# A decoder layer on one Trainium2 core: all transposing DMAs issued by ScalarE instead of SyncE

## The chip, the core and the metric

The kernel runs on one core of one Trainium2 chip. The metric is the device time of one execution, in microseconds (us); lower is better. Engines are named as the profile names them: PE (TensorE, with its weight loads as PEld), DVE (VectorE), ACT (ScalarE), POOL (GpSimd) and SP (SyncE, which here does nothing but issue DMAs and wait). "SPq" and "ACTq" mark DMA issues.

## What is computed

A pre-norm decoder layer on x of shape (16, 256, 256): 16 blocks (index b) of 256 rows, model width 256. Cut to what matters:

```python
x = x + attn(layernorm(x))            # one head, width 256, causal, linear position bias
x = x + xattn(layernorm(x), ctx)      # 16 heads of 16, keys and values from ctx (16, 256, 256)
x = x + moe(layernorm(x))             # 8 experts, top 2, F = 1024

def moe(x):                           # x: 4096 rows
    p = softmax(x @ w_gate)           # (.., 8); the best two are kept and scaled to sum 1
    g, u = split(x @ w_gate_up[e])    # per expert, 256 -> 2 * 1024
    y = (silu(g) * u) @ w_down[e]     # 1024 -> 256
    return sum of p[e] * y[e] over the two chosen experts
```

All is float32 in and out. Inside, most products are made of float16 halves: a value is split in a high half and the rest, and three products are added.

## The kernel before

It is written directly per engine: five instruction streams, with semaphores between them, and the order in each stream is written out by hand.

**Attention part** (0 to about 490 us). A software pipeline over the 16 blocks: `iteration(b, ...)` on every engine handles the front of block b+2 (norms, self-attention, projections: functions `f_...`), the head work of blocks b and b+1 (`h_...`) and the tail of block b-1 (`t_...`: output projection, third norm, gate logits, top two, and ranks). In the same iterations the expert weights are split into halves (`split_hi` on ACT, `split_lo` on POOL) and stored to memory, three pieces an iteration. The iterations in the loop take 28.2 us each.

The gate of a block needs its normed rows transposed. The path is: variance (DVE) -> `rsqrt_tail` (POOL L767) -> `t_norm3` (DVE L1344) -> `t_xn3`, the high half (ACT L1101, helper L1000) -> `xn3_rest`, the low half (POOL L807, semaphore xn3_lo) -> `transpose_normed` (SP L427 to 434, a transposing DMA of 256 KB from xn3_h to xn3_t) -> `t_gate` (PE L2241, matmul line L2246), which sits at a fixed place between the head matmuls in PE's order. SP also issues all loads and stores in a fixed order around it: `load_pieces`, `store_stream`, `transpose_normed`, `load_next`, `store_pieces`, `stack_rows`, `stack_k_hi` and so on, `store_normed` last.

**Expert part** (about 490 us to the end). The 8192 (row, expert) pairs are sorted into 68 slots of 128 rows; four streams j = 0..3 take slots in turn, so slot s belongs to stream s % 4. For slot s:
- SP loads the slot's entries (L579), DVE makes row numbers (`slot_rows`, L1929), POOL gathers the 128 rows with an indirect DMA (`gather`, L893, semaphore rows_in), SP transposes them with a DMA (`transpose_rows`, L615, semaphore rows_t_in), PE multiplies.
- In SP's `slot(s)` (L656): once PE has finished the gate and up products of slot s (gu_ps), it waits for the gathered rows of slot s+4, issues their transposition, and then loads the weights of slot s+4 (2 MB `load_gate_up` L527, 1 MB `load_down` L531; only where the expert changes), and after that entries for slot s+8. At three points in the loop and once at its end `load_second` loads another 3 MB, for the last four slots.
- PE's `slot` runs four steps f = 0..3; a step is `gate_up(s, f)` (24 matmuls, L2477) and a `down` of two steps earlier (6 matmuls, L2507): after `gate_up(s, 2)` comes `down(s, 0)`, after `gate_up(s, 3)` comes `down(s, 1)`.
- ACT's `slot` (L1276) per step: `silu` of step f (L1282), then `act_round` of step f-1 (L1000, act_hi), and in odd streams a `result` at f = 2 (L1264). DVE makes act_t (L1976) and act_lo (L1923). `down(s, f)` waits for act_lo of step f.
- POOL alternates `gather(s+4)` and `scatter_results(s)` (L913, adds a slot's results to `out` in memory; each waits for the one before to have landed).

Between the two parts stand `before_last` (block 14's heads) and `last_attention` (block 15's), whose tails run in part beside the first slots (`last_tail`).

## Time and profile before

| | us |
|---|---|
| three timed runs | 1106.5, 1101.28, 1106.62 (median 1106.5) |
| the profiled execution | 1098.74, span 1097.0 |
| PE busy | 1003.0 (91%) |
| DVE, ACT, POOL busy | 643.0 (59%), 627.1 (57%), 536.1 (49%) |
| mean granted PE clock | 0.975 of full |

The profile comes from one execution, which is a little faster than the three timed ones. The busy shares are means over two parts that differ: in the attention iterations ACT is busy for nine tenths of the time, in the expert part for under four tenths. Such shares say little of a change in one place; the stretches and the waits in the section on rows are what to read. In a timeline a line is: start, duration, engine, source line, operation, output <- input, count, and in brackets the engine's idle time before it with what ended it. DMA issues show the time in which the issuing engine writes them out, not the transfer.

### The profile page before, as it was taken

What the parts mean: (1) busy time and instruction counts of PE and PEld (TensorE: products, weight loads), DVE (VectorE), ACT (ScalarE), POOL (GpSimd) and SP (SyncE); (2) the same over time, 40 slices, a digit from 0 to 9 for tenths busy, and PEclk for the clock granted to TensorE, in tenths of its full rate; (3) what the DMA queues carried; (4) which work ended last, traced back from release to release, by engine and by line L of the source; (5) the groups of instructions that cost most, each with busy time, mean ns of one, the idle gap of its engine ahead of it and who ended that gap; (6) DMA issues with size and microseconds to landing.
All of it is one profiled execution on the core that took longest, in us unless ns stands there. A gap on an engine that the chain in (4) does not pass through costs nothing.

```text
span 1097.0 us, 36445 instructions
## 1 busy us (share of the span) xinstructions
PE 1003.0 (91%) x12720; PEld 834.7 (76%) x12720; DVE 643.0 (59%) x2077; ACT 627.1 (57%) x1343; POOL 536.1 (49%) x580
## 2 busy tenths in 40 slices
PE   5689899999999999765999999999999999999984
PEld 4356666666666666423988999999999999999974
DVE  6667788888888887752456444444444444444422
ACT  6589898988888888644343333333333333334321
POOL 6756777777777777413244232233323232333313
PEclk9799999999999999987999999999999999999998
DMA  5855656656666663359543455854664752235791
GB/s 191 269 179 177 161 173 183 184 188 186 192 192 192 193 194 118 108 138 285 165 70 49 62 157 166 265 132 93 170 160 98 231 161 52 48 52 158 231 301 18
DMA packets 146817, 173.95 MB, mean 159 GB/s; under 512 B 75072, under 2 KB 123264, under 8 KB 141888
## 3 DMA queue, kind: packets, MB, share of 16 engines
q1 hardware_dynamic: 131486, 154.95, 45.9%
q0 software_dynamic: 15248, 18.18, 9.9%
q8 instruction: 35, 0.57, 0.3%
q14 instruction: 30, 0.25, 0.1%
q10 hardware_dynamic: 18, 0.01, 0.0%
HBM read 270.75 MB, written 43.07 MB: 286 GB/s over the span
## 4 chain that ended last, share of the span: by engine, by line
PE 61%; DVE 12%; DMA 11%; issue 7%; POOL 4%; ACT 2%; another core or an unknown queue 1%; SPq 1%; DVEq 0%; ACTq 0%; POOLq 0%
PE front L2477 14%; PE t_ring L2477 14%; PE pv L2507 7%; PE s_ring L2507 7%; DMA out<-y_sb,place_i 5%; DMA xn_t<-xn_h 4%; PE pv L2204 3%; PE front L2045 3%; PE s_ring L2171 3%; PE front L2054 2%; PE t_ring L2189 2%; DVE nmax L1417 2%; DVE stats L1326 2%; POOL entries L770 1%; POOL xn_h L807 1%
## 5 line engine op out<-in xcount | busy, mean ns | idle before, releaser
L913 POOL DMA_INDIRECT out<-y_sb,place_i x64 | 100.3, 1568 | 279.4 <-ACT y_sb L1264 81.0
L2477 PE MATMUL t_ring<-rows_t,wgu_sb 128*128 128x128 f16 x3072 | 194.0, 220 | 0.0
L2477 PE MATMUL front<-rows_t,wgu_sb 128*128 128x128 f16 x3072 | 192.5, 219 | 0.0
L2477 PEld LDWEIGHTS t_ring<-rows_t,wgu_sb 128*128 128x128 f16 x3072 | 183.8, 98 | 2.9
L2477 PEld LDWEIGHTS front<-rows_t,wgu_sb 128*128 128x128 f16 x3072 | 182.1, 98 | 3.8 <-issue 0.8
L1083 ACT ACTIVATE probs_t<-t_ring,mask_bias 128x512 f32<-128x512 f32 x256 | 164.7, 699 | 31.9 <-PE t_ring L2189 30.1
L1417 DVE TENSOR_REDUCE nmax<-s_ring 128x2 f32<-128x512 f32 x256 | 166.0, 685 | 14.5 <-PE s_ring L2171 12.3
L1282 ACT ACTIVATE silu_g<-t_ring 128x256 f32<-128x256 f32 x136 | 52.3, 385 | 169.4 <-PE t_ring L2477 152.1
L1282 ACT ACTIVATE silu_g<-front 128x256 f32<-128x256 f32 x136 | 51.9, 383 | 166.1 <-PE front L2477 144.2
L1976 DVE SCALAR_TENSOR_TENSOR act_t<-t_ring,silu_g 128x256 f32<-128x256 f32 x136 | 57.7, 425 | 151.5 <-ACT silu_g L1282 138.0
L1976 DVE SCALAR_TENSOR_TENSOR act_t<-front,silu_g 128x256 f32<-128x256 f32 x136 | 57.6, 424 | 146.4 <-ACT silu_g L1282 142.2
L814 POOL TENSOR_TENSOR w_halves<-w_scaled,w_halves 128x256 f16<-128x256 f32 x192 | 122.3, 670 | 12.1 <-ACT w_scaled L1116 11.8
L1000 ACT ACTIVATE act_hi<-act_t 128x256 f16<-128x256 f32 x272 | 111.5, 410 | 15.6 <-DVE act_t L1976 15.3
L1923 DVE TENSOR_TENSOR act_lo<-act_t,act_hi 128x256 f16<-128x256 f32 x272 | 114.4, 421 | 1.3 <-issue 1.2
L893 POOL DMA_INDIRECT rows<-normed,row_i x68 | 68.3, 1004 | 88.7 <-DVE row_i L1929 59.1
L2507 PE MATMUL pv<-wd_sb,act_hi 128*128 128x256 f16 x512 | 104.8, 273 | 2.3 <-issue 1.1
L2507 PE MATMUL s_ring<-wd_sb,act_hi 128*128 128x256 f16 x512 | 105.5, 274 | 1.6 <-DVE act_lo L1923 1.6
L2171 PE MATMUL s_ring<-k_stack,q_stack 128*128 128x256 f16 x512 | 93.5, 285 | 8.0 <-DVE nmax L1417 4.1
L2189 PE MATMUL t_ring<-q_stack,k_stack 128*128 128x256 f16 x512 | 88.3, 276 | 7.2 <-ACT probs_t L1083 5.8
L2171 PEld LDWEIGHTS s_ring<-k_stack,q_stack 128*128 128x128 f16 x512 | 42.8, 99 | 53.0 <-DVE nmax L1417 27.9
L2204 PE MATMUL pv<-probs_t,v_aug 128*32 128x256 f32 x1024 | 78.3, 398 | 0.0
L791 POOL TENSOR_TENSOR xn_h<-xn_t,xn_h 128x512 f16<-128x512 f32 x32 | 37.4, 1168 | 81.1 <-ACT xn_h L1019 69.0
(307 smaller groups left out, 1855.6 us busy)
## 6 DMA issues: line engine op xcount, KB each, us to landing
wgu_sb<-gu_split SPq DMA_DIRECT2D x68, 2048.0 KB
wd_sb<-down_split SPq DMA_DIRECT2D x68, 1024.0 KB
w_piece<-in_w_gu SPq DMA_DIRECT2D x32, 512.0 KB, 4.6
gu_split<-w_halves SPq DMA_DIRECT2D x32, 512.0 KB, 3.8
w_piece<-in_w_down SPq DMA_DIRECT2D x16, 512.0 KB, 6.3
down_split<-w_halves SPq DMA_DIRECT2D x16, 512.0 KB, 4.4
x_in<-in_x SPq DMA_DIRECT2D x16, 256.0 KB, 2.9
ctx_in<-in_ctx_t_in SPq DMA_DIRECT2D x16, 256.0 KB, 3.0
```

Of the source, the lines that this page charges most:

```text
L814: o = nc.gpsimd.tensor_tensor(w_halves[:, i, 1, c:c + LOCKED], w_scaled[:, i, c:c + LOCKED], w_halves[:, i, 0, c:c + LOCKED], ALU.subtract)
L1000: return nc.scalar.activation(to, frm, ACT.Copy)
L1083: nc.scalar.activation(probs_t[:, g % 2, r], t_ring[r][:].rearrange("p (j q) -> p j q", j=2), ACT.Exp, bias=mask_bias[:, g % 2, bass.ds(b, ...
L1282: nc.scalar.activation(silu_g[:, f % 2], gu_ring[f][:, 0:2 * SLOT], ACT.Silu, scale=1 / (WSCALE * RSCALE)).then_inc(silu_sb, 1)
L1417: nc.vector.tensor_reduce(nmax[:, n // HJ, :, n % HJ], s_ring[n % 2][:].rearrange("p (r k) -> p r k", r=2), AX.X, ALU.max, negate=True).th ...
L1923: nc.vector.tensor_tensor(act_lo[:, f], act_t[:, f % 2], act_hi[:, f], ALU.subtract).then_inc(alo_sb, 1)
L1976: nc.vector.scalar_tensor_tensor(act_t[:, f % 2], gu_ring[f][:, 2 * SLOT:4 * SLOT], ASCALE / (WSCALE * RSCALE), silu_g[:, f % 2], ALU.mult ...
L2171: o = nc.tensor.matmul(s_ring[n % 2][:, r * S:(r + 1) * S], q_stack[:, p, j, qt * P:(qt + 1) * P], k_stack[:, p, r, j], start=True, stop=True)
L2189: o = nc.tensor.matmul(t_ring[r][:, jj * S:(jj + 1) * S], k_stack[:, p, r, 2 * jp + jj, kt * P:(kt + 1) * P], q_stack[:, p, 2 * jp + jj], ...
L2204: o = nc.tensor.matmul(pv[q:q + 32, 0:S], v_aug[:, p, kt, HJ * r + 2 * jp + jj], probs_t[:, g % 2, r, jj], start=(kt == 0), stop=(kt == 1))
L2477: o = nc.tensor.matmul(gu_ring[f][:, part * SLOT:(part + 1) * SLOT], wgu_sb[j][:, w, at:at + P], rows_t[:, j, NC * r + c], start=(i == 0), ...
L2507: o = nc.tensor.matmul(down_banks[j % 2][:, 0:D], a[:, f, k * SLOT:(k + 1) * SLOT], wd_sb[j][:, w, tile_ * D:(tile_ + 1) * D], start=(tile ...
```

## The change

Every transposing DMA leaves SP's stream and goes into ACT's, as `t_turn` (gates) and `turn_rows` (expert rows), with the same waits in front:

```diff
 # ACT
+            def t_turn(c, p):
+                act.wait_ge(xn3_lo, c + 2)
+                act.sem_inc(act_passed, 1)
+                act.wait_ge(gate_ps, c + 1)
+                act.sem_inc(act_passed, 1)
+                nc.scalar.dma_start_transpose(xn3_t[:].rearrange("p t a n -> p (t a) n"),
+                                              xn3_h[:, p].rearrange("p t d -> p (t d)")).then_inc(xn3t_in, 16)
+            def turn_rows(j, g):
+                act.wait_ge(rows_in[j], 16 * g + 16)
+                act.sem_inc(act_passed, 1)
+                nc.scalar.dma_start_transpose(rows_t[:, j], rows[:, j]).then_inc(rows_t_in[j], 16)
 # ACT, iteration
                     h_exp(b, 3, 0)
                     h_exp(b, 3, 1)
+                    h_out(b, p, 0)
                 if c:
                     t_xn3(b - 1, 1 - p, h + p - 1)
-                if t:
-                    h_out(b, p, 0)
                 if f:
                     split_hi(b + 2, 2, p, h + 2)
+                if c:
+                    t_turn(b - 1, 1 - p)
                 if t:
                     h_exp(b, 4, 0)
...
 # ACT, slot: behind silu(s, 1) and act_round(s, 0)
+                    if f == 1 and more:
+                        turn_rows((j - 1) % STREAMS, g + (1 if j else 0))
 # ACT, last_attention and last_tail
+                    if g in (0, 2):
+                        turn_rows(g // 2, 0)
+                    if g == 6:
+                        t_turn(b - 1, 0)
...
+                if s == 0 and f in (2, 3):
+                    turn_rows(f, 0)
+                if s == 3 and f == 2:
+                    t_turn(B - 1, 1)
 # SP, iteration
                     load_pieces(b + 3, h + 1 + p, 1 - p)
-                if c:
-                    store_stream(b - 1)
-                    transpose_normed(b - 1, 1 - p)
                 if f and (not isinstance(b, int) or b + 4 < B):
                     load_next(b + 4, p)
+                if c:
+                    store_normed(b - 1, 1 - p)
+                    store_stream(b - 1)
...
-                if c:
-                    store_normed(b - 1, 1 - p)
 # SP, slot
                     sp.wait_ge(gu_ps, FP * s + FP)
-                    transpose_rows(j, g + 1)
                     load_gate_up(e, j, new)
 # SP, ahead of the slots
             sp.wait_ge(exp_sb, 16 * (B - 1))
-            transpose_rows(0, 0)
-            transpose_rows(1, 0)
...
             load_stream(2)
-            transpose_rows(2, 0)
-            transpose_rows(3, 0)
             load_stream(3)
 # POOL, iteration
+                if parted:
+                    scatter_part(p, 2)
                 if c:
                     rsqrt_tail(b - 1)
-                if parted:
-                    scatter_part(p, 2)
-                    scatter_part(p, 3)
+                if n:
+                    rsqrt_norm1(b + 3)
                 if c:
                     xn3_rest(b - 1, 1 - p)
...
+                if parted:
+                    scatter_part(p, 3)
```

In slot s, ACT thus turns the rows of slot s+3 (stream j-1), at step 1; SP turned those of slot s+4 once slot s had its gate and up products. The order of the iteration is written anew on the other engines too: on PE `h_values`, `h_scores` and `h_scores_t` change places by one or two (the gate product `t_gate` now follows `h_scores_t(5, 1)` and `h_scores(12, 14)`, ahead of `h_values(4)` and `h_scores_t(6, 0)`), on DVE `t_norm3` comes one `h_max` later and the two `t_recip` stand together, on ACT `t_gate` comes ahead of `h_exp(6, ..)`. In the first fronts (the pipeline's filling) weights, copies and loads of blocks 0 and 1 are ordered anew on all engines. No arithmetic is added or removed.

## Rows read from the trace of the kernel before

**Rows 1.** Stretches: length, busy us (and instructions) per engine, PE clock, DMA share, GB/s.
```profile
244.70:272.90 28.20, 27.00 (x257) 18.96 (x255) 23.43 (x76) 25.38 (x48) 21.86 (x27) 1.00 0.65 187
...
481.20:484.00 2.80, 2.76 (x27) 1.29 (x28) 1.53 (x7) 1.48 (x3) 0.77 (x1) 0.50 0.03 11
...
620.00:1020.00 400.00, 400.00 (x6016) 386.35 (x6014) 176.80 (x576) 152.79 (x427) 128.66 (x100) 1.00 0.52 136
```
**Rows 2.** Waits of SP's own queue: us in total, times, longest.
```profile
SPq L614 <- DMA rows<-normed,row_i: 185.9, 49, 10.3
```
**Rows 3.** Single source lines of DMA issues: duration ns min/median/max, first and last start.
```profile
L433 SPq DMA_TRANSPOSE xn_t<-xn_h x16: 1274/1318/3480, 101.0 to 550.5; - x16
...
DMA to landing us min/median/max: 3.1/3.2/10.4
...
L615 SPq DMA_TRANSPOSE rows_t<-rows x68: 1197/1226/3821, 490.7 to 1048.4; - x68
...
L1294 ACTq DMA_DIRECT2D q_stack<-nmax_t x1: 1270/1270/1270, 488.0 to 488.0; - x1
...
L518 SPq DMA_DIRECT2D q_stack<-nmax_t x15: 662/667/727, 57.5 to 453.8; - x15
```
**Rows 4.** Timeline of one attention iteration around the gate's transposition, POOL, ACT, SP.
```profile
243.41 1.18 POOL L807 TENSOR_TENSOR xn_h<-o_n,xn_h 128x512 f16<-128x512 f32 x1
...
244.02 1.06 ACT L1116 ACTIVATE w_scaled<-w_piece 128x1024 f32<-128x1024 f32 x1
...
244.78 1.31 SPq L433 DMA_TRANSPOSE xn_t<-xn_h  x1
```
**Rows 5.** Timeline of PE at three of the 16 gate products.
```profile
248.03 0.46 PE L2246 MATMUL tail<-wg_split,xn_t 128*128 128x8 f16 x12 [0.19 <-DMA xn_t<-xn_h]
...
481.24 0.48 PE L2246 MATMUL tail<-wg_split,xn_t 128*128 128x8 f16 x12 [5.49 <-DMA xn_t<-xn_h]
...
515.14 0.48 PE L2246 MATMUL tail<-wg_split,xn_t 128*128 128x8 f16 x12 [9.05 <-DMA xn_t<-xn_h]
```
**Rows 6.** Timeline of an ordinary slot, steps 1 and 2, all engines.
```profile
840.42 1.00 POOL L893 DMA_INDIRECT rows<-normed,row_i  x1 [0.46 <-issue]
...
842.20 0.41 ACT L1000 ACTIVATE act_hi<-act_t 128x256 f16<-128x256 f32 x1
...
843.25 1.22 SPq L615 DMA_TRANSPOSE rows_t<-rows  x1
...
843.92 0.38 ACT L1282 ACTIVATE silu_g<-t_ring 128x256 f32<-128x256 f32 x1 [1.31 <-PE t_ring L2477]
...
844.67 0.41 DVE L1923 TENSOR_TENSOR act_lo<-act_t,act_hi 128x256 f16<-128x256 f32 x1
...
844.86 0.35 SPq L527 DMA_DIRECT2D wgu_sb<-gu_split  x1
...
845.71 0.27 PE L2507 MATMUL pv<-wd_sb,act_hi 128*128 128x256 f16 x1
```
**Rows 7.** The next slot, whose rows come late: POOL, ACT, SP.
```profile
848.38 1.00 POOL L893 DMA_INDIRECT rows<-normed,row_i  x1 [0.74 <-issue]
...
851.90 0.38 ACT L1282 ACTIVATE silu_g<-t_ring 128x256 f32<-128x256 f32 x1 [1.31 <-PE t_ring L2477]
...
856.56 1.21 SPq L615 DMA_TRANSPOSE rows_t<-rows  x1
```
**Rows 8.** Timeline: an early slot with late rows, SP and ACT.
```profile
577.73 0.38 ACT L1282 ACTIVATE silu_g<-t_ring 128x256 f32<-128x256 f32 x1 [0.98 <-PE t_ring L2477]
...
579.60 1.22 SPq L615 DMA_TRANSPOSE rows_t<-rows  x1
```
**Rows 9.** SP's timeline: first and last transposition with late rows between 620 and 1020.
```profile
641.29 1.24 SPq L615 DMA_TRANSPOSE rows_t<-rows  x1
...
1000.39 1.24 SPq L615 DMA_TRANSPOSE rows_t<-rows  x1
```

160 lines of the change are left out of this document (73 added, 87 removed).

## The prediction

> **What bounds the kernel now.** I read first the stretches, then the waits of SP's queue, then single iterations and slots in the timeline. The stretches [rows 1] show two parts. In an attention iteration of 28.2 us PE is busy for 27.0 and ACT for 25.4: PE sets the pace and ACT stands close behind, with 2.8 us free. From 620 to 1020 PE is busy for all of 400 us, 50 slots of 8.0 us; ACT works 153 us there. So in the expert part nothing but PE matters, as long as nobody keeps PE waiting. SP waited there for gathered rows 49 times, 185.9 us in all and up to 10.3 at once [rows 2], and PE did not notice: SP has nothing behind that wait that is needed within three slots. The change gives this wait to ACT, whose next instruction is the silu that PE needs two microseconds later. That is the centre of the forecast.
>
> **Expert slots, the wait.** In slot s ACT will stand at `turn_rows` after silu of step 1 and act_round of step 0. Take the ordinary slot [rows 6]. ACT is through with that at 842.61 (842.20 + 0.41). The rows were gathered from 840.42 and SP, which waits for nothing else, issued at 843.25; so ACT waits 0.6 us, then issues for 1.22 us, to 844.47. Its silu of step 2 was at 843.92: 0.55 us late. What is late next: act_lo of step 1 ended at 845.08 (844.67 + 0.41) and PE's `down` that needs it began at 845.71, so 0.63 us are free. 0.55 against 0.63: an ordinary slot costs PE nothing, or a tenth or two where act_lo is a little later. For some 35 ordinary slots I enter +2 us.
>
> A late slot is another matter [rows 7]. Its gather was issued at 848.38 and its rows were there only when SP issued at 856.56, 8.2 us later instead of 2.8, beside 3 MB of expert weights issued from 844.86 [rows 6]. ACT would be free of the issue at 857.77, its silu was due at 851.90: 5.87 late, less 0.63 free, 5.2 us of PE standing. PE has only one step of gate and up products to do meanwhile, and that is in the 0.63. The same subtraction over all slots from 620 to 1020 gives nine groups of neighbouring late slots, the first with the issue at 641.29 and the last at 1000.39 [rows 9]; counted by the latest of each group, since once PE has stood the next rows come in time, they are 4.6 to 6.9 us each, **51 us** together. SP will issue a slot's weights some 5 to 7 us earlier, as it no longer waits for the rows. That moves the burst onto the slot's own gather instead of the next one's: a gather begun some 2 us after the weights, as at present one begun 3.5 us after them, is late all the same. I keep nine; between a half (25) and eleven bursts (60).
>
> Before 620 the slots 1 to 9 have late rows for other reasons (POOL has the last tails). At 579.60 SP issued for a slot whose silu of step 2 was at 577.73 [rows 8]: 579.60 + 1.22 - 577.73 - 0.63 = 2.5. Four such slots give 8 to 11; SP itself was late in one, so +6, bounds 0 and 10.
>
> **The clock behind a stop.** After the 5.49 us in which PE waited at 481 [rows 5] the granted clock stood at half in 481.2 to 484.0 [rows 1], so 2.8 us gave 1.4 us of work. Nine stops of like length may each do this. Not all will, as some are shorter: +1 us each, **+9**, bounds 0 and 20.
>
> **Attention iterations.** Removed: SP's wait and issue. Added: the same on ACT. ACT's last activation ahead of it, the third `split_hi`, ends at 245.08; SP issued at 244.78 and needed 1.31 us [rows 4]. On ACT the issue comes right behind, to about 246.3, and the exponentials of group 4 come 1.3 us later. ACT has 2.8 us free an iteration [rows 1], but PE waits for these exponentials, and the new order puts only one or two more score products (0.27 us each) ahead of them. The gate's transposition starts up to 0.5 us later and takes 3.2 us to land [rows 3]; PE's gate product had waited 0.2 us in this iteration [rows 5] and is at about the same place. POOL's single scatter less ahead of `xn3_rest` gains little, because ACT's high half, now behind `h_out`, comes 0.3 us later. Bounds: minus 1.2 (all that PE is idle in an iteration) and plus 1.3 (ACT's issue in full). I take +0.5, nearer to ACT's side, as two engines over 26 of 28.2 us get in each other's way; for 13 iterations **+6.5**, bounds -15 and +17.
>
> The Trainium skill, "Perfetto Trace Analysis", section "Per-engine timelines", says that an engine's sequencer pushes an activation to a queue and goes on to the next instruction, while a DMA is executed by the sequencer. Then the issue would run beside the `split_hi` still at work and the term would be 0 or a gain, the sum 6.5 us lower. No row here shows an ACT issue behind a running activation, so this is not in the sum. In a slot it would change nothing, since ACT is idle there when the rows come.
>
> The other way round: ACT's one DMA issue took 1.27 us, where the same transfer from SP took 0.67 [rows 3]. If transpositions cost ACT 0.6 more than SP's 1.23, every slot goes over its 0.63. That is a rival below.
>
> **Between the parts.** The gate products of blocks 13 and 14 waited 5.49 and 9.05 us [rows 5]. The second wait is for a transposition that stood in SP's queue behind 3 MB of weights, which SP had issued late since it waited for rows first; one such took 10.4 us to land instead of 3.2 [rows 3]. From ACT it doesn't stand behind them, and the weights go 4 to 7 us earlier. Most of the 9.05 should go; late next are ACT's own issues, three of 1.2 us in `last_attention`, and the gathers of rows 2 and 3. Net **-8**, bounds -13 and +3 (the transfer shares the engines with the next weights). At 481 nothing changes. First fronts anew: a different order of the same work, 0, bounds ±3. The end: a chain of result scatters behind the last slots, the same length, 0, bounds ±5.
>
> **Sum.** On the profiled execution's 1098.7: + 6.5 (iterations) - 8 (between) + 6 (early slots) + 2 (ordinary) + 51 (late) + 9 (clock) = 1165.2. The profiled execution lies 2.5 to 8 us under the three timed runs, so I add 3: **1168**.
>
> **Rivals.**
> - *ACT's waits are shorter than SP's were.* Part of the late rows come earlier because results are scattered earlier or the burst misses the gather; half of the late term, no clock loss: 1098.7 + 6.5 - 8 + 6 + 25 + 3 = 1131. For it: the lateness is set by where a burst of 10 us falls against a gather every 8 us. Against: a gather between -1.5 and +5 us of a burst's start was late each time, and the new place is inside.
> - *The rows are in time (the other side).* If the gather lands before ACT is there plus 0.7 us in nearly all slots, the expert part costs nothing; the iterations give back PE's idle 1.2 us each (-15) and the stop between the parts goes (-8): 1098.7 - 23 + 3 = 1079. It decides from there on: late rows under 0.7 us. Against: rows 7 and 9.
> - *ACT issues slowly*, by the 1.27 against 0.67: 0.6 us more in some 58 slots (35) and 13 iterations (8): 1168 + 43 = 1211.
> - *It doesn't tell*: gains between and in the iterations offset a small loss in the slots, 1102 to 1111.
> The Trainium skill, "DMA: Bandwidth & Descriptors", section "Issuing engines are not separate DMA queues", says that starting DMAs on several engines saves only the sequencer's time for it, which is usually small. By it the 186 us of SP's waiting buy nothing; the trace agrees as far as PE was never short of weights from 620 to 1020.
>
> **How the numbers follow.** Forecast 0.58, shorter waits 0.20, slow issue 0.08, the other side 0.09, no difference 0.05. Half a per cent, 5.5 us, is about what a measurement of this kernel can tell from no change. Faster: 0.09. Within 0.5%: 0.05. Slower: 0.86. Range for 8 in 10: from 1115 (shorter waits at their low end) to 1200 (late term 60, clock 20, iterations +12 and ordinary slots +5 over their values).
>
> **What would show it.** Late slots: in the profile after, ACT's silu of step 2 preceded by idle time that a gather's DMA ended, PE idle ahead of `down` behind act_lo for 4 to 7 us some nine times, and PE busy under 0.9 of the expert part. Clock: half level behind these. Iterations: a period of 28.7 us. Between: the gate product of block 14 waiting under 3 us. Wrong would be: PE still busy without a gap from 620 on, or ordinary slots over 8.3 us.

## The result, and the profile after

The changed kernel takes 1276.94 us (median of four runs, 1275.25 to 1283.97) where the kernel before took 1103.89 in the same comparison (1098.99 to 1106.62): a ratio of 1.1585, interval 1.1519 to 1.1652. It was forecast slower, at 1168, with a range to 1200. The direction held; 109 us are missing from the forecast. (One execution of j_gate_first below, 1677.64 us at a granted clock of 0.56, lies apart from its nine others and is in no ratio.) The profiled execution has a span of 1276.3 us, PE is busy for 84% of it and its mean granted clock is 0.917.

The stretches of the profile after, one attention iteration and the expert part that answers to [rows 1]; columns as there:

```profile
301.50:335.60 34.10, 29.76 (x257) 19.99 (x256) 23.84 (x76) 25.66 (x48) 21.85 (x26) 0.90 0.51 155
...
620.00:1020.00 400.00, 351.74 (x4930) 330.04 (x4928) 158.62 (x548) 126.62 (x352) 115.26 (x90) 0.94 0.46 114
```

The same 257 PE instructions that took an iteration of 28.2 us now take 34.1. ACT does hardly more work than before (25.66 against 25.38 us), so it isn't short of time. Of the 5.9 us more, 3.1 are PE idle; 2.8 are PE busy for longer with the same instructions, and its granted clock is 0.90 where it was 1.00. In the expert part PE stands for 48 of 400 us, where it had stood for none.

Three places carry the difference: the iterations, the part between, and the slots. They are measured between the same instructions of both traces: the issues of the gate's transposition of blocks 0 and 13, the first `silu` of slot 0, and the first `silu` of the last slot.

| stretch | before | after | difference | forecast |
|---|---|---|---|---|
| 13 attention iterations | 375.0 | 433.2 | +58 | +6.5 |
| block 13's transposition to slot 0 | 42.3 | 57.2 | +15 | -8 |
| slots 0 to 13 | 114.1 | 133.7 | +20 | +6 |
| slots 13 to 60 | 375.1 | 448.4 | +73 | +62 |
| slots 60 to 67 | 66.5 | 77.1 | +11 | 0 |

(The forecast's 62 are its 51 for late slots, 9 for the clock and 2 for ordinary slots.)

**A late slot.** The timeline after, ACT, POOL, SP and PE of one slot; columns: start, duration, engine, line, what, in brackets the idle time before it and what ended it:

```profile
711.55 0.34 SPq L518 DMA_DIRECT2D wgu_sb<-gu_split  x1
...
714.32 1.01 POOL L871 DMA_INDIRECT rows<-normed,row_i  x1 [0.30 <-issue]
...
716.24 0.41 ACT L978 ACTIVATE act_hi<-act_t 128x256 f16<-128x256 f32 x1
720.56 1.22 ACTq L1260 DMA_TRANSPOSE rows_t<-rows  x1
721.95 0.38 ACT L1281 ACTIVATE silu_g<-t_ring 128x256 f32<-128x256 f32 x1 [5.30 <-issue]
...
723.18 0.39 PE L2510 MATMUL s_ring<-wd_sb,act_hi 128*128 128x256 f16 x1 [3.27 <-DVE act_lo L1923]
```

This is the picture forecast from [rows 7]. (POOL L871 is the gather, L891 the scatter; L1281 is ACT's `silu`, L1260 its `turn_rows`.) The gather was issued 2.8 us behind the weights' issue and came 6.2 us later; ACT was free at 716.65 and issued at 720.56, its `silu` was at 721.95, and PE ran out of work and waited for act_lo. It waited for it 31 times in this part (the waits of PE from 620 to 1180; columns: us in total, times, longest):

```profile
PE pv L2510 <- DVE act_lo L1923: 45.0, 23, 6.7
PE s_ring L2510 <- DVE act_lo L1923: 16.0, 8, 3.7
```

**An attention iteration.** PE's scores for ACT's next exponentials; ACT's timeline after, around the gate's transposition; and PE's gate product of this iteration and of block 14:

```profile
301.42 0.60 PE L2189 MATMUL t_ring<-q_stack,k_stack 128*128 128x256 f16 x4
...
300.91 1.04 ACT L1103 ACTIVATE w_scaled<-w_piece 128x1024 f32<-128x1024 f32 x1
301.48 1.26 ACTq L1087 DMA_TRANSPOSE xn_t<-xn_h  x1
303.01 1.26 ACT L1061 ACTIVATE probs_t<-t_ring,mask_bias 128x512 f32<-128x512 f32 x2 [1.07 <-PE t_ring L2189]
...
308.23 0.21 ACT L1092 ACTIVATE gexp<-logits 128x16 f32<-128x16 f32 x1 [2.52 <-DVE logits L1488]
309.53 1.26 ACT L1061 ACTIVATE probs_t<-t_ring,mask_bias 128x512 f32<-128x512 f32 x2 [1.09 <-PE pv L2204]
...
307.29 0.48 PE L2246 MATMUL tail<-wg_split,xn_t 128*128 128x8 f16 x12 [2.48 <-DMA xn_t<-xn_h]
...
590.18 0.48 PE L2246 MATMUL tail<-wg_split,xn_t 128*128 128x8 f16 x12 [4.37 <-DMA xn_t<-xn_h]
```

ACT's issue begins at 301.48, while the activation that ends at 301.95 still runs. That settles one question of the forecast: the issue does go beside a running activation. The Trainium skill has it so in "Perfetto Trace Analysis", section "Per-engine timelines". But then ACT stood for 1.07 us, to 303.01. The bracket names PE's t_ring, which had ended at 302.02 (301.42 + 0.60); the issue ended at 302.74. So most of the 1.07 is the issue's, and it was not free. The other new thing is the landing: from the issue at 301.48 to the product at 307.29 are 5.8 us, and PE waited 2.48 of them, where it had waited 0.19 [rows 5]. The transposition itself is the same, 1.26 us to issue from either engine; "ACT issues slowly" is out. It is on another queue now (q10 in the page's part on queues; SP's q1 keeps the rest):

```profile
q1 hardware_dynamic: 77598, 141.83, 33.4%
...
q10 hardware_dynamic: 53906, 13.13, 6.1%
```

53906 packets for 13.13 MB are 244 bytes each; these small packets become the thread of this study.

The stop has a second part. The first line below is PE behind its wait of 2.48 us; the others are 12 iterations, from the gate's transposition of block 0 to that of block 12, before and after:

```profile
307.29:313.00 5.71, 5.71 (x42) 2.84 (x42) 2.50 (x7) 3.02 (x7) 1.80 (x2) 0.50 0.62 237
```
```profile
101.04:443.53 342.49, 325.69 (x3068) 227.38 (x3064) 281.53 (x897) 305.18 (x565) 262.74 (x312) 1.00 0.61 179
```
```profile
103.06:502.67 399.61, 348.69 (x3062) 236.52 (x3063) 282.04 (x896) 308.30 (x565) 260.84 (x310) 0.92 0.50 154
```

Behind the wait the granted clock stood at half for 5.7 us. The 12 iterations grew by 57.1 us. In the trace the granted clock is at half for 61.4 of their 399.6 us, and at no time in those of before. PE was busy for 56.7 of those 61.4, with work that takes at least half as long at the upper level. So at most 28 of the 57.1 us are the clock's (an estimate from these two numbers); the rest is PE waiting.

**Between the parts.** The chain of what ended last (start, us, what) and the timeline of ACT and PE in the last attention block:

```profile
553.22 18.84 DMA rows<-normed,row_i
```
```profile
572.15 1.22 ACTq L1260 DMA_TRANSPOSE rows_t<-rows  x1
573.41 0.38 ACT L978 ACTIVATE o_t<-pv 128x256 f32<-128x256 f32 x1 [16.14 <-issue]
...
573.94 1.08 PE L2204 MATMUL pv<-probs_t,v_aug 128*32 128x256 f32 x8 [16.22 <-ACT o_t L978]
```

ACT waits for slot 1's rows in the middle of block 15's heads. The gather shares the transfer engines with three loads of SP issued from 550.66 to 552.30 (4 MB) and takes 18.8 us where an ordinary slot's took 2.8 [rows 6]. ACT's next copy stands behind it, and PE behind the copy: 16.2 us of new wait, against 4.7 taken off block 14's gate product (9.05 to 4.37). That leaves 11.5 of the +15. The stretch in question (columns as above) shows PE busy for 4.43 of 18.9 us, at a mean granted clock of 0.59:

```profile
553.20:572.10 18.90, 4.43 (x32) 2.13 (x24) 0.00 (x0) 3.09 (x6) 3.11 (x3) 0.59 0.88 214
```

The forecast wrote -8 here.

### The profile page after: what moved, and what is told of

It is laid out like the page before. It is cut to its first block, busy times and chain, and to the rows that moved or that the text cites. A ratio compares the mean times of both kernels' runs of the same rounds, so it can differ in the third digit from the quotient of the medians.

```text
span 1276.3 us, 36453 instructions
## 1 busy us (share of the span) xinstructions
PE 1065.9 (84%) x12720; PEld 865.7 (68%) x12720; DVE 643.7 (50%) x2077; ACT 629.1 (49%) x1343; POOL 539.5 (42%) x580
## 3 DMA queue, kind: packets, MB, share of 16 engines
q10 hardware_dynamic: 53906, 13.13, 6.1%
## 4 chain that ended last, share of the span: by engine, by line
PE 30%; DMA 27%; issue 14%; POOL 9%; ACT 7%; DVE 6%; ACTq 6%; POOLq 1%; DVEq 0%
DMA rows<-normed,row_i 18%; DMA xn_t<-xn_h 7%; ACTq L1260 5%; PE front L2480 4%; PE pv L2204 4%; PE front L2045 3%; PE t_ring L2189 3%; POOL out L891 3%; POOL w_halves L791 3%; PE pv L2510 2%; PE front L2054 2%; PE t_ring L2480 2%; PE s_ring L2171 2%; DMA out<-y_sb,place_i 2%; PE front L2032 2%
## 5 line engine op out<-in xcount | busy, mean ns | idle before, releaser
L891 POOL DMA_INDIRECT out<-y_sb,place_i x64 | 102.0, 1593 | 387.7 <-ACT y_sb L1254 170.5
L2480 PE MATMUL front<-rows_t,wgu_sb 128*128 128x128 f16 x3072 | 208.8, 229 | 0.0
L2480 PEld LDWEIGHTS front<-rows_t,wgu_sb 128*128 128x128 f16 x3072 | 197.5, 103 | 7.2 <-issue 1.2
L1281 ACT ACTIVATE silu_g<-t_ring 128x256 f32<-128x256 f32 x136 | 52.1, 383 | 235.8 <-issue 125.8
L2510 PE MATMUL pv<-wd_sb,act_hi 128*128 128x256 f16 x512 | 113.6, 288 | 62.8 <-DVE act_lo L1923 62.8
L1281 ACT ACTIVATE silu_g<-front 128x256 f32<-128x256 f32 x136 | 52.0, 383 | 203.4 <-PE front L2480 186.5
L1976 DVE SCALAR_TENSOR_TENSOR act_t<-front,silu_g 128x256 f32<-128x256 f32 x136 | 57.6, 424 | 183.1 <-ACT silu_g L1281 181.7
L2510 PE MATMUL s_ring<-wd_sb,act_hi 128*128 128x256 f16 x512 | 108.5, 279 | 16.4 <-DVE act_lo L1923 16.0
L978 ACT ACTIVATE act_hi<-act_t 128x256 f16<-128x256 f32 x272 | 112.0, 412 | 18.7 <-DVE act_t L1976 18.3
L2171 PE MATMUL s_ring<-k_stack,q_stack 128*128 128x256 f16 x512 | 100.6, 291 | 10.3 <-DVE nmax L1422 6.5
L2189 PE MATMUL t_ring<-q_stack,k_stack 128*128 128x256 f16 x512 | 97.4, 299 | 13.6 <-ACT probs_t L1061 12.9
L2204 PE MATMUL pv<-probs_t,v_aug 128*32 128x256 f32 x1024 | 92.7, 450 | 16.2 <-ACT o_t L978 16.2
L2510 PEld LDWEIGHTS pv<-wd_sb,act_hi 128*128 128x128 f16 x512 | 52.6, 103 | 74.7 <-DVE act_lo L1923 68.1
L871 POOL DMA_INDIRECT rows<-normed,row_i x68 | 68.3, 1005 | 78.6 <-DVE row_i L1929 48.3
```

The costliest lines, as they stand in the source:

```text
L891: nc.gpsimd.indirect_dma_start(out=out, out_offset=bass.IndirectOffsetOnAxis(ap=place_i[:, j:j + 1], axis=0), in_=y_sb[:, j], in_offset=No ...
L978: return nc.scalar.activation(to, frm, ACT.Copy)
L1976: nc.vector.scalar_tensor_tensor(act_t[:, f % 2], gu_ring[f][:, 2 * SLOT:4 * SLOT], ASCALE / (WSCALE * RSCALE), silu_g[:, f % 2], ALU.mult ...
L2171: o = nc.tensor.matmul(s_ring[n % 2][:, r * S:(r + 1) * S], q_stack[:, p, j, qt * P:(qt + 1) * P], k_stack[:, p, r, j], start=True, stop=True)
L2189: o = nc.tensor.matmul(t_ring[r][:, jj * S:(jj + 1) * S], k_stack[:, p, r, 2 * jp + jj, kt * P:(kt + 1) * P], q_stack[:, p, 2 * jp + jj], ...
L2204: o = nc.tensor.matmul(pv[q:q + 32, 0:S], v_aug[:, p, kt, HJ * r + 2 * jp + jj], probs_t[:, g % 2, r, jj], start=(kt == 0), stop=(kt == 1))
```

## Experiments

Theory going in: (1) ACT's waits for rows, with the number of late slots larger than counted, make the slots' loss; (2) in the iterations the cost is not ACT's issue alone but the transfer on a second queue, which is late beside SP's traffic. The main rival for (2): the new order of the iteration, not the queue. In all of these a "long slot" is one of over 10 us between slots 13 and 60, by the `silu` lines of ACT's timeline; the period is the mean of the first 12 intervals between the gate's transpositions. The us of the table are those of each version's profiled execution. In the ten versions below that leave the expert part as it was (b, c, d, m, n, p, u, v, x, y), slots 0 to 67 take 551.9 to 558.5 us, so a few us there say nothing.

| kernel | period | long slots | other slots, mean | slots 0 to 67 |
|---|---|---|---|---|
| before | 28.5 | 0 | 7.98 | 555.7 |
| after | 33.3 | 9 of 14.3 | 8.41 | 659.2 |
| a_rows_act | 28.5 | 9 of 14.2 | 8.39 | 658.4 |
| b_gates_act | 33.6 | 0 | 7.98 | 557.1 |
| c_gates_act_old_order | 30.6 | 0 | 7.98 | 557.6 |
| d_new_order_sp | 30.0 | 0 | 7.98 | 558.5 |
| h_rows_wait_only | 28.5 | 10 of 13.6 | 8.11 | 627.6 |
| f_rows_act_later | 28.5 | 5 of 12.9 | 8.09 | 605.9 |
| g_rows_act_weights_wait | 28.5 | 10 of 13.8 | 8.37 | 656.0 |
| r_rows_act_no_bursts | 28.5 | 3 of 15.3 | 8.42 | 627.2 |
| t_rows_later_no_bursts | 28.4 | 0 | 7.98 | 566.8 |

### The change in halves

a_rows_act: the expert part and the last two blocks of the changed kernel, the iterations of before.

```diff
+            def turn_rows(j, g):
+                act.wait_ge(rows_in[j], 16 * g + 16)
+                act.sem_inc(act_passed, 1)
+                nc.scalar.dma_start_transpose(rows_t[:, j], rows[:, j]).then_inc(rows_t_in[j], 16)
...
+                    if f == 1 and more:
+                        turn_rows((j - 1) % STREAMS, g + (1 if j else 0))
```

> The kernel before, with the changed kernel's expert part and its last two attention blocks: ACT issues the transpositions of the expert rows and of the last gates, while the iterations up to block 13 stay as before. Theory 1, the parts add up: the slots bring +100 to +105 us as in the changed kernel and the stretch between the parts 0 to +15, so 1200 to 1225 us, with PE standing in some 15 slots of over 12 us. Theory 2, the late slots come from the later and longer attention part (other timing of the tails): then the slots bring the forecast's 60 to 70 us only, 1165 to 1175 us.

b_gates_act is the complement: ACT issues the gates' transpositions of blocks 0 to 12, in the new order; rows and last gates by SP.

> The complement: iterations and first fronts of the changed kernel (ACT issues the gates' transpositions, new order), expert part and its rows by SP as before. Theory 1: the iterations keep their period of 33.5 us against 28.2, +55 to +65 us, and the slots stay at 8.0 us: 1160 to 1170 us. Theory 2, part of the iteration's loss is brought in by something that the expert part does: not possible before 480 us, so a period under 32 us would say that it is the tails of blocks 13 to 15. The stop of 9.05 us ahead of block 14's gate product should be back here (SP's queue).

Measured: a_rows_act 1209.75 us (ratio 1.1022, 1.0953 to 1.109), b_gates_act 1164.42 (1.0609, 1.0517 to 1.07), beside 1097.79 for before. +112.0 and +66.6 make 178.6; the whole change made 173.1. The halves add up within the intervals, so they can be studied alone. a_rows_act has the same nine long slots and the same 8.39 us for the others as the changed kernel: nothing of the slots' loss comes from the attention part. Its between-part wait is there too (`pv` behind `o_t`, 10.9 us once). b_gates_act has the period and nothing else.

### The iterations: order, queue or issue

c_gates_act_old_order moves only the issue, into the old order; d_new_order_sp has only the new order.

```diff
 # c: ACT, iteration
                     split_hi(b + 2, 2, p, h + 2)
+                if c:
+                    t_turn(b - 1, 1 - p)
 # c: SP, iteration
-                    transpose_normed(b - 1, 1 - p)
+                    if isinstance(b, int) and b >= 14:
+                        transpose_normed(b - 1, 1 - p)
```

> The kernel before with one edit: in the iterations ACT issues the gate's transposition behind its third split_hi, SP does not; the order of all else is the old one. Theory 1, the issue from another queue costs (the transposition takes 5.5 us to land instead of 3.2, since SP's loads and stores now run beside it): the period grows by 3 to 5 us an iteration, +40 to +65 us. Theory 2, the new order costs: +0 to +10 us here.

> The other half of that edit: the changed kernel's new order of first fronts and iterations, with SP issuing the gates' transpositions ahead of its loads as before, and the expert part as before. Theory 1 (the queue costs): 0 to +10 us, a period of 28.2 to 29 us. Theory 2 (the order costs, the gate's exponential on ACT now ahead of the sixth exponential and the gate product there on PE): most of the +58 us, 1145 to 1165 us.

Measured: c 1128.76 (1.0284, 1.0236 to 1.0332), d 1115.42 (1.0162, 1.0073 to 1.0251). Neither theory alone. c gives 31 us, under its forecast of 40 to 65. d gives 17.6, with 8 to 28 in its interval, where "order harmless" said at most 10 and a period up to 29; the period of 29.95 says so more clearly than the time. Together 48.6 of the 66.6; 18 us belong to neither alone. ACT's timeline in c:

```profile
286.03 1.06 ACT L1126 ACTIVATE w_scaled<-w_piece 128x1024 f32<-128x1024 f32 x1
286.73 1.26 ACTq L1110 DMA_TRANSPOSE xn_t<-xn_h  x1
288.27 1.27 ACT L1084 ACTIVATE probs_t<-t_ring,mask_bias 128x512 f32<-128x512 f32 x2 [1.18 <-issue]
```

Here the exponentials' input was there; ACT lost 1.18 us to its own issue. The transpositions' time from issue to landing (min/median/max) in c and, below it, in b:

```profile
DMA to landing us min/median/max: 3.1/5.1/9.3
```
```profile
DMA to landing us min/median/max: 3.2/6.0/10.1
```

Before it was 3.1/3.2/10.4 [rows 3], and in d it is 3.1/3.2/10.3. So the landing is late only from ACT's queue. In c the gate product waits 0 to 1.2 us for it, since PE, held by ACT's issue, comes later itself; in b it waits 1.2 to 3.4 us for it.

Two pairs took the sharing away: SP holds its loads and stores of the iteration back, until PE has done the gate product (m on c, n on b), or only until the transposition has landed (v on c, u on b).

```diff
 # SP, iteration; m and n: sp.wait_ge(gate_ps, b + 1)
+                if c and not (isinstance(b, int) and b >= 14):
+                    sp.wait_ge(xn3t_in, 16 * (b - 1) + 48)
+                    sp.sem_inc(sp_passed, 1)
                 if f and (not isinstance(b, int) or b + 4 < B):
                     load_next(b + 4, p)
```

> c_gates_act_old_order with one wait more: SP issues its next loads and stores of an iteration only when PE has done the gate product, so that nothing of SP's runs beside the transposition from ACT's queue. Theory 1, the sharing of the transfer engines makes the landing late (5.1 us against 3.2): it is back at 3.2 to 3.5 us, and the period falls from 30.6 to 29 to 29.5 us; ACT's issue (1.2 us) stays: 1108 to 1118 us. Theory 2, the queue of ACT is slow by itself: landing still about 5 us and the time not under that of c_gates_act_old_order, 1128 us, or above it by what SP loses.

> b_gates_act with the same wait of SP. Theory 1 (sharing): landing from 6.2 back to about 3.3 us, PE's gate product waits under 1 us instead of 2 to 3.4, and the period of 33.5 to 34 comes down to 30.5 to 31.5 us: 1120 to 1135 us. Theory 2 (the order and ACT's issue, not the transfer): within 10 us of b_gates_act, 1155 to 1170 us.

> m_old_order_sp_held with the shorter hold: SP's next loads and stores wait for the transposition's landing only, not for PE's product, so SP is released 1 to 2 us earlier. Theory 1, in m_old_order_sp_held the landing was mended (3.1 us) and the time lost again since SP's own later work came late: 10 to 20 us less than its 1136 us, that is 1116 to 1126, under c_gates_act_old_order. Theory 2, sharing was never the cost in the old order, ACT's 1.2 us issue is: 1125 to 1136 us.

> n_new_order_sp_held with the same shorter hold. Theory 1 (sharing costs in the new order, where the product stands 3.2 us behind the issue): 1125 to 1138 us, 4 to 17 us under n_new_order_sp_held. Theory 2: at or over its 1142 us.

| kernel | us | over its own before | period | landing, median |
|---|---|---|---|---|
| c, old order | 1128.8 | 31.0 | 30.6 | 5.1 |
| m, held to the product | 1135.8 | 38.2 | 31.7 | 3.1 |
| v, held to the landing | 1117.9 | 23.5 | 30.6 | 3.1 |
| b, new order | 1164.4 | 66.6 | 33.6 | 6.0 |
| n, held to the product | 1142.3 | 44.7 | 32.0 | 3.1 |
| u, held to the landing | 1132.5 | 38.1 | 31.3 | 3.1 |

(The median of the kernel before beside these is 1097.79 us for c and b, 1097.57 for m and n, 1094.36 for v and u; so the second column is the one to compare.)

The landing came back to 3.1 us in all four, from ACT's queue as from SP's. The queue isn't slow by itself; what runs beside it is the cause, as theory 1 had it. What that is worth depends on the order. In the new order it is 28 us (b to u: 2.3 an iteration). Most of it is not the wait itself but the clock behind it: within 12 iterations PE was busy at half clock for 57.6 us in b and for 10.1 in u. By the same estimate that makes up to 2.0 of the 2.3. In the old order no gain shows in the period: c and v both have 30.6. Against m, v is 15 us faster, 1.1 an iteration, as expected of the shorter hold. That it would also be under c for want of sharing isn't shown: the intervals of the two ratios (1.0236 to 1.0332, 1.0139 to 1.0281) overlap. The longer hold cost SP's next work, as PE's waits show in n (from 160 to 400):

```profile
PE t_ring L2201 <- DMA q_stack<-nmax_t: 13.3, 7, 2.8
```

p_gates_wait_only gives ACT the waits alone:

```diff
+            def t_wait(c, p):
+                act.wait_ge(xn3_lo, c + 2)
+                act.sem_inc(act_passed, 1)
+                act.wait_ge(gate_ps, c + 1)
+                act.sem_inc(act_passed, 1)
```

> The kernel before; ACT has only the two waits of the gate's transposition behind its third split_hi (the low halves written, the last gate product done), SP issues the transposition as before. Theory 1, ACT's waits are short in the iterations (the low half is written about when the third split_hi ends) and its issue is what delays the exponentials: 0 to +5 us, period 28.2 to 28.5. Theory 2, it is the wait that holds ACT: a period of 29 to 30.5 us as in c_gates_act_old_order, +15 to +31 us.

1095.19 against 1094.36 (ratio 0.9996, 0.998 to 1.0013), period 28.5: the waits cost nothing. So in the old order the 2.0 us of period (c minus p) are the issue on ACT and what follows from it; v, without the sharing, has as much, but with whatever the hold costs in it.

Last, which engine's new order makes d's 1.4 us of period: x puts DVE's order in the iterations back, y puts PE's back.

> d_new_order_sp (the new order alone, SP issuing, +17.6 us) with VectorE's order in the iterations put back. In d_new_order_sp PE's main new wait was for VectorE's maxima (s_ring behind nmax, 7.3 us in 8 iterations), and those of its waits that are longer than before sum to about 1.2 us an iteration. Theory 1, it is VectorE's order that costs: a period of 28.2 to 28.6, 1095 to 1103 us. Theory 2, it is the order of PE's products: over 1110 us as in d_new_order_sp.

> d_new_order_sp with PE's order in the iterations put back instead. Theory 1 (VectorE's order costs): over 1110 us. Theory 2 (PE's order costs): 1095 to 1103 us. If both x_order_dve_old and this one stay over 1108, it is what they share: the order on ScalarE, SP and GpSimd.

x 1133.34 (1.0306, 1.0245 to 1.0367), y 1138.76 (1.0355, 1.029 to 1.042): both slower than d. PE's largest waits from 160 to 400 in x and in y:

```profile
PE s_ring L2185 <- DVE nmax L1431: 19.9, 23, 1.9
```
```profile
PE front L2041 <- DVE xn L1358: 13.8, 8, 1.8
```

With either engine's old order put back alone, a wait comes up that is larger than what was sought: the orders of PE and DVE fit each other only in pairs. The experiment is inconclusive: by its own rule both over 1108 would point to the order that they share, on ACT, SP and GpSimd, but the new waits above are between PE and DVE. Which engine's order costs d its 1.4 us stays open.

### The slots: wait, issue or transfer

h_rows_wait_only is the kernel before with the wait alone on ACT; SP still issues.

```diff
+                    if f == 1 and more:
+                        act.wait_ge(rows_in[(j - 1) % STREAMS], 16 * (g + (1 if j else 0)) + 16)
```

> The kernel before with one instruction more on ACT in each slot: behind the silu of step 1 ACT waits until the next slot's rows are gathered, as the changed kernel's turn_rows does. SP still waits and issues the transposition itself. Theory 1, the wait alone stops ACT: nine groups of late rows, each 1.2 us less than in the forecast since no issue follows (3.4 to 5.7 us each), some 40 us, with the clock behind the stops 50: 1140 to 1155 us. Theory 2, the cost lies in the issue on ACT or in the transfers' new queue: under 10 us, 1098 to 1108 us.

1169.94 us, ratio 1.0643 (1.0591 to 1.0696): +73 us, over the 50 expected, from one instruction that issues nothing and moves nothing. ACT's and PE's waits from 620 to 1080:

```profile
ACT silu_g L1282 <- DMA rows<-normed,row_i: 63.8, 12, 7.7
```
```profile
PE pv L2509 <- DVE act_lo L1925: 28.7, 7, 5.7
```

Ten long slots between 13 and 60 and 8.11 us for the others. So the wait is the larger part of the slots' +103. The rest (a minus h, 31 us in slots 0 to 67) comes when the issue follows it: ordinary slots 8.39 instead of 8.11, and 17 us in slots 0 to 13. In slots 0 to 13 a differs from h by the first slots' and the last gates' transpositions as well, so not all 17 need be the issues in the slots.

f_rows_act_later keeps the issue on ACT and takes the wait's reason away: ACT turns the rows gathered one slot earlier.

```diff
-                        turn_rows((j - 1) % STREAMS, g + (1 if j else 0))
+                        turn_rows((j - 2) % STREAMS, g + (1 if j >= 2 else 0))
```

> The rows by ACT as in a_rows_act, but ACT turns the rows that are gathered one slot earlier: it issues for the slot after next, whose gather has had 8 us more, so it need not wait; the issue itself stays, 68 times. Theory 1, the wait is the cost: the slots come back to 8.0 us but for the start, +10 to +25 us over before (1108 to 1125 us; the tails of the last attention blocks stay as in a_rows_act). Theory 2, the issue or the queue is the cost: within 20 us of a_rows_act, 1190 to 1210 us.

1161.27 us (1.0564, 1.051 to 1.0619): neither, and the most telling miss. ACT no longer waited, ordinary slots went to 8.09 us, and still five were long. PE's chain from 716 to 737 (start, us, what) says why, and the queues' packets from 724 to 736 (packets, MB, share of 16 engines' time) say how:

```profile
719.53 17.01 DMA rows_t<-rows
```
```profile
q1 hardware_dynamic: 321, 1.95, 76.4%
q10 hardware_dynamic: 366, 0.09, 4.8%
```

The transposition landed 17.0 us after its issue. It was issued 12 us before PE needed it, in time by any landing seen before ([rows 3] has 3.2 for the larger one), but SP's weights ran beside it. In twelve microseconds SP's queue moved 321 packets and ACT's 366: nearly one for one, but SP's packets carry 6 KB on average and ACT's 250 bytes. The issue on another engine had put the transposition beside the weights; on SP's queue it stands ahead of them and is through before they begin. This is a case where the Trainium skill had the rule and I didn't weigh it: "DMA: Bandwidth & Descriptors", section "Queues, rings and completion order", says that each transfer engine goes round the queues that have work, packet by packet. The trace agrees as far as the packets counted in the profile go, with 321 against 366, and block 14's transposition below shows it again.

g_rows_act_weights_wait puts the place of the burst back (SP waits for the slot's rows before it issues the weights, as before); r and t take the bursts away.

```diff
 # g: SP, slot
+                    sp.wait_ge(rows_in[j], 16 * (g + 1) + 16)
                     load_gate_up(e, j, new)
 # r (on a) and t (on f): the mark for a new expert compares a slot's expert with itself
-                                            slot_ec[:, EARLY - STREAMS:NSLOT - STREAMS], ALU.not_equal
+                                            slot_ec[:, EARLY:NSLOT], ALU.not_equal
```

> a_rows_act with one edit: SP, as before, waits for the gathered rows of the slot before it issues a slot's weights, so that a burst of weights no longer falls onto the slot's own gather. Theory 1, the forecast's number of late slots was too small because the burst moved: nine groups again instead of 15, so 30 to 45 us less than a_rows_act, 1165 to 1180 us. Theory 2, every burst of weights catches some gather, wherever it starts, and a stop delays all alike: within 10 us of a_rows_act, 1200 to 1215 us.

> a_rows_act without the expert weights' bursts: the mark that a slot's expert differs from that of four slots earlier is always 0, so that SP loads no weights from slot 4 to 61 (the experts computed with are wrong there, the work of every engine is the same). Theory 1, bursts make the gathers late: no slot over 10 us between 13 and 60, and what stays is the ordinary slot's 8.35 us: 75 to 90 us less than a_rows_act, 1120 to 1135 us. Theory 2, POOL's own chain (scatter, gather) makes them late: at least half of the long slots stay, over 1165 us.

> f_rows_act_later without the bursts, in the same way. In f_rows_act_later ACT did not wait and still seven slots of some 13.5 us stood, behind transpositions that landed 17 us after their issue. Theory 1, these landed late because ACT's queue shares the transfer engines with SP's 8 and 16 KB packets: without bursts no long slot is left and slots are 8.0 us, 40 to 50 us less, 1112 to 1122 us. Theory 2, a transposition from ACT's queue is late for another reason: long slots stay, over 1145 us.

g: 1207.49 us (1.0985, 1.0905 to 1.1065), within noise of a_rows_act; ten long slots against nine. Between these two places the burst's start makes no difference; theory 2 was right, and my belief that the burst's new place had made more late slots was wrong. The changed kernel has nine in slots 13 to 60, as forecast; the expectation's 15 took in slots outside that stretch.

t: 1125.48 us (1.026, 1.0113 to 1.0407), with PE busy without a gap in the expert part:

```profile
620.00:1020.00 400.00, 400.00 (x6016) 386.36 (x6014) 177.40 (x577) 153.19 (x428) 129.76 (x101) 1.00 0.36 73
```

So some 50 transpositions issued by ACT cost PE nothing there: the issue on ACT is free in a slot if ACT need not wait ahead of it. The lateness in f went with the weights' bursts. Three bursts are left in t, those of `load_second`, and here they hit no transposition that PE was waiting for. (The two executions are 1118.93 and 1132.02 us, their median a little over the 1112 to 1122 expected: between the parts PE still waits 12.0 us once behind ACT's `o_t`, and slots 60 to 67 take 72.9 us.)

r: 1179.25 us (1.0751, 1.0613 to 1.0888), 30 us less than a_rows_act, not the 75 to 90 expected. By its time it lies with theory 2 (over 1165 us), but what the traces show is neither: six long slots went, three stayed, and slots 0 to 13 and 60 to 67 kept their loss. The three begin at 735.0, 843.3 and 951.5. In r three loads of weights are left between slots 13 and 60, those of `load_second`; two of them (columns of a source line: duration ns min/median/max, first and last start):

```profile
L607 SPq DMA_DIRECT2D wgu_b<-gu_split x2: 343/345/347, 840.1 to 948.3; - x2
```

The first is at 731.8. Every long slot that stayed follows one of the three bursts that stayed. The early slots' loss is not that of the bursts behind slot 4: slots 0 to 13 take 134.1 us in r and 133.9 in a.

The ordinary slot kept 8.42 us without bursts, so its +0.4 is not the burst's either. The chain of what ended last shows what it is. In the changed kernel, from 765 to 782 (start, us, what; L1254 is ACT's copy of the result before, `result`):

```profile
765.07 2.83 DMA rows<-normed,row_i
...
768.00 1.21 ACTq L1260
...
769.95 0.47 ACT y_sb L1254
...
771.31 1.13 POOL out L891
...
773.25 2.71 DMA rows<-normed,row_i
...
781.75 2.75 DMA rows<-normed,row_i
```

PE isn't in it, nor in what the dots leave out. The gather lands, ACT issues the transposition, and only behind that copies the last result; POOL scatters the result and then issues the next gather, for which ACT waits again. Every second time DVE makes the copy. This ring of ACT and POOL takes 8.2 and 8.5 us from gather to gather, and PE's work for a slot takes 8.0, so the ring sets the pace. It closes by the wait and is too long by the issue in it: in h, which lacks the issue, and in t, which lacks the wait, the chain from 915 to 930 runs through PE's products alone.

### Block 14's gate, the gain that was forecast

s_block14_by_act: the kernel before, this one transposition by ACT, behind the exponentials of group 6.

```diff
+                    if g == 6:
+                        act.wait_ge(rows_t_in[0], 16)
+                        act.wait_ge(rows_t_in[1], 16)
+                        t_turn(b - 1, 0)
 # SP, ahead of the row transpositions of slots 2 and 3
+            sp.wait_ge(xn3t_in, 16 * (B - 2) + 48)
```

> The kernel before, with block 14's gate transposition alone issued by ACT (in the last attention block behind its exponentials of group 6; it waits for the two row transpositions of SP, which landed long before), so that it doesn't stand behind 3 MB of weights in SP's queue. If that queueing is the stop of 9.05 us, it falls to 3 to 4.5 us, and the kernel gains 3 to 6 us (ratio 0.995 to 0.997). If ACT's place behind group 6 is as late as the queue was, or the transposition shares the engines with the weights, it stays within 2 us of before.

1111.53 us, ratio 1.0157 (1.0131 to 1.0182): 17 us slower where a gain of 3 to 6 was expected. (The profiled execution, 1104.68 us, is the fastest of the five and 10 us over before; the other 7 are in no trace.) The chain, PE's gate product, and the queues from 517 to 523:

```profile
506.16 18.26 DMA xn_t<-xn_h
```
```profile
524.47 0.48 PE L2261 MATMUL tail<-wg_split,xn_t 128*128 128x8 f16 x12 [17.00 <-DMA xn_t<-xn_h]
```
```profile
q1 hardware_dynamic: 213, 2.33, 92.1%
q10 hardware_dynamic: 217, 0.06, 4.1%
```

In SP's queue this transposition stood behind 3 MB and took 10.4 us [rows 3]; on a queue of its own it took 18.3, as it now shares not with those 3 MB alone but with all that SP issues after them. In the profiled execution slot 0 comes 52.4 us behind block 13's issue instead of 42.3, which is about all of its 10 us. 217 packets of ACT's queue went against 213 of SP's in six microseconds, 0.06 MB against 2.33; from 506 to 525, about the whole transfer, it is 1056 against 1074. The edit also makes SP wait for the landing before it turns the rows of slots 2 and 3, at 524.52 instead of 514.12; slots 0 to 13 take 110.8 us (111.3 in p_gates_wait_only, beside the same runs of before), so that wait shows no cost there.

j_gate_first instead keeps it on SP's queue and moves the weights behind it:

```diff
-            load_stream(1)
             iteration(15, 1, 7, True, True, False, False, False)
+            load_stream(1)
```

> The kernel before with one edit: SP issues the second stream's expert weights behind the loads of block 15 rather than ahead of them, so that the gate's transposition of block 14 does not stand behind 3 MB of weights. If that queueing makes the stop of 9.05 us, it goes to under 2 us and the kernel is 5 to 9 us faster (1090 to 1094 us where before is at 1098). If the stop is made by something else (the row's own chain, PE's order), the time stays within 2 us; if the weights of stream 1 are now late for slot 1, it is slower by 3 to 8 us.

1094.79 us against 1096.98, ratio 0.9968 (0.9943 to 0.9993). PE's gate product of block 14:

```profile
508.02 0.46 PE L2246 MATMUL tail<-wg_split,xn_t 128*128 128x8 f16 x12 [2.40 <-DMA xn_t<-xn_h]
```

The stop of 9.05 us is 2.40, where under 2 was expected, but the gain is 2 us by the medians and 3.5 by the ratio, not 5 to 9. Of the 6.7 us taken off, 2.1 come back at PE's next wait, behind DVE's `chosen` (4.1 us at most instead of 2.0), and slot 0 comes 4.3 us earlier against block 13's issue (38.0 against 42.3). The slots' 557.6 us instead of 555.7 are within their spread. A third of a per cent is left. It is the one version here whose whole interval lies under 1.

## Why the forecast was wrong, point by point

**"In the expert part nothing but PE matters", and the wait on ACT: right.** The mechanism is the one that happened, in the slots between 13 and 60 to the number: nine long slots were forecast and nine came. Their size came out close: they are 14.3 us long against 7.98, so 57 us together, where 51 and 9 for the clock had been entered. h_rows_wait_only shows the wait alone to be the larger part.

**Ordinary slots: mis-sized.** 0.55 us late against 0.63 free was to cost "nothing, or a tenth or two". It was 0.43 each (8.41 minus 7.98), 38 times: 16 us instead of 2. The step that failed is the slack: 0.63 us ahead of PE's `down` was all that was compared. ACT's lateness also holds back its copy of the last result, so the scatter, so the next gather, for which ACT waits again; the ring takes 8.2 and 8.5 us against PE's 8.0. A slack read off one slot doesn't tell of a loop over several. "Ordinary slots over 8.3 us" stood as a mark of being wrong; they were.

**Early slots: +20 instead of +6; the last ones +11 instead of 0.** The forecast took 6 where it had worked out 8 to 11. What makes the 20 is shown in part: the wait alone gives 3 (h, 117.1 against 114.1, little outside the spread of 110.6 to 115.8 in the versions with the old expert part), the issue without the wait 6 (f, 120.5), both together 20 (a), as much in r, with no burst between slots 4 and 13. And the last slots were left out of the count of late ones, as the count went over PE's full stretch only ([rows 9], 620 to 1020), while `load_second` and the last experts' weights come behind it: the two slots of 17.2 and 16.1 us among the last are the longest of all (the longest of them was 14.0 before).

**Iterations: the step that failed most, 58 us against 6.5.** Three terms by the runs, in us an iteration: the new order 1.4 (d, 29.95, minus before, 28.54), the issue on ACT 1.4 (u, 31.32, minus d; what the hold costs is in it), the sharing of the transfer engines 2.3 (b, 33.59, minus u). If the hold costs anything, the issue's share is smaller by that and the sharing's larger. They sum to b's 5.1; the changed kernel has 4.8. The forecast had one of the three, at 0.5 between bounds of -1.2 and 1.3, where 1.3 was "ACT's issue in full". In the old order the issue took 2.0 of period for 1.2 us of standing (c, p), so the upper bound was too low even for this term alone. What it left out is the clock. The forecast entered the granted clock behind PE's stops in the slots and not in the iterations. By the estimate above it makes up to 0.9 of c's 2.0 (PE busy at half clock for 21.9 us in 12 iterations) and up to 2.4 of the changed kernel's 4.8 (56.7 us). The new order was "one or two more score products", not priced by itself. (The reason given for +0.5, two engines "over 26 of 28.2 us", had ACT too high: it is at 25.4 [rows 1].) And "takes 3.2 us to land [rows 3]" was carried over from SP's queue to ACT's, the same transfer: there it took 5.1 us (c) and 6.0 (b) in the median. In the old order no cost of it shows in the period, in the new order it is 2.3 us, for which the order alone leaves no room: d's gate product stands just where a landing of 3.2 us ends.

**Between the parts: the wrong sign, +15 against -8.** "From ACT it doesn't stand behind them" is true and didn't help: out of SP's queue is into the sharing, which s_block14_by_act shows to be dearer (17.0 us of wait against 9.05). In the changed kernel the product's wait did fall, to 4.37, but not for the reason given: the wait for slot 1's rows, 16.2 us of PE, had put the transposition off to 584.35, 32 us behind the issue of the last weights and 3 ahead of the next (587.14), and it landed in 5.8 us. That wait was the unpriced step: `last_attention` has `turn_rows` for slots 0 and 1 in the midst of the exponentials, and the rule used for the slots (gather beside a burst, ACT behind it, PE behind ACT) held there too. I counted three issues of 1.2 us and not what they wait for.

**The rivals.** "Shorter waits" and "the rows are in time" fell with the first trace. "ACT issues slowly" fell too: 1.26 and 1.21 us, as from SP. The sentence on the sequencer was right as to the issue beside a running activation (301.48 against 301.95) and wrong in what I hung on it, "0 or a gain": the issue is 1.26 us, what was left of the activation 0.47. The Trainium skill's "DMA: Bandwidth & Descriptors", section "Issuing engines are not separate DMA queues", says that issuing on several engines saves only the sequencer's time. That holds here as to the gain: no version in which ACT issues is faster than before. The move cost 2.3 us an iteration by the sharing (b to u), and 17 us where one transposition was moved beside weights (s).

**The range.** Its upper end, 1200, is less than its own terms give: 1168 + 9 + 11 + 12 + 5 = 1205. The result lies outside either way.

**Still open:** which engine's order makes d's 1.4 us; how much of u's and v's period the hold itself costs; what makes the early slots' 20 us out of a wait and an issue that cost 3 and 6 alone; and the 7 us of s that are in no trace.

## What to carry to other kernels

Before a wait is moved to an engine, ask what that engine must do within the longest wait on record, everywhere that the wait is issued: waits that cost nothing on SP (49, 185.9 us) cost 73 us by one instruction on ACT. Ask too what that engine does behind the wait, and whether the thing waited for depends on it, one round later. If so, add up the ring and compare it with the pace (8.2 and 8.5 us against 8.0 here). And where PE is made to stop often, price the clock behind the stops as well as the stops. In these runs a transfer of small packets was in time ahead of a burst in the same queue and late on a queue of its own beside it: where it stands behind a burst, move the burst (j, 0.3% faster), not the transfer (s, 1.6% slower). A duration from issue to landing belongs to the queue and to the company it was measured in; it can't be carried to another queue as it stands.

## What the runs showed of the hardware

- Two queues with work shared the transfer engines about one packet for one, though the packets differed by a factor of forty: 213 packets of 11 KB on average against 217 of some 256 bytes (s, 517 to 523). A transposition of 256 KB took 3.1 us from either queue with SP's loads and stores held back, 4.4 to 6.7 us beside them in the changed kernel's iterations, and 18.3 us beside weights.
- A gather of 128 rows, from its issue to the transposition that waited for it, went from 2.8 us to 6.2 in a slot and 18.8 beside 4 MB of weights.
- ACT's issue of a transposing DMA takes 1.26 us and starts while an activation runs, but ACT then stood for 1.07 us (the changed kernel) and 1.18 (c); in a slot with ACT idle it cost PE nothing (t: some 50 of them in a stretch in which PE was busy for all 400 us).
- The granted clock was at its upper level over the whole of t's 400 us and at a mean of 0.94 in the changed kernel's, where PE stopped again and again: the 14.3 us of a long slot hold the clock's share as well. In an iteration it stood at half for 5.7 us behind a stop of PE of 2.48 us.
